# A layer of gated cross-attention and routed experts: the second norm kept as two half-precision parts, an experts' tile's rows transposed by a crossbar DMA

## The reference

```
# x (8, 256, 256), ctx (8, 120, 256), 16 heads of 64; all f32
x = x + tanh(g_xattn) * xattn(layernorm(x), ctx, w_q, w_kv, w_out, b_out)
x = x + tanh(g_ffn)   * ffn(layernorm(x), W1, W2, Wr)

# ffn over T = 2048 rows, E = 8 experts, DFF = 1024, TOPK = 2
probs = softmax(x @ Wr.T);  vals, idx = top_k(probs, 2);  gate = vals / vals.sum
h   = silu(einsum('btd,efd->btef', x, W1))
y   = einsum('btef,edf->bted', h, W2)
out = einsum('bte,bted->btd', gate, y)
```

## Time and profile before

| | us |
|---|---|
| median of 3 runs | 574.97 |
| lowest, highest run | 567.21, 582.94 |
| span of the profiled execution | 560.1 |
| TensorE busy in it | 493.7 |
| VectorE, ScalarE, GpSimd busy | 370.2, 371.3, 363.9 |
| DMA traffic | 93.13 MB, mean 166 GB/s |

### The profile page before, as it was taken

One profiled execution on the slowest core, in us unless ns is written; L12 is line 12 of the kernel. 1 busy time (PEld: TensorE's weight loads), 2 busy tenths in 40 slices (PEclk: granted clock), 3 DMA queues, 4 the chain that ended last, 5 costly groups with the idle time before them and its releaser, 6 DMA issues. The chain is left out here.

```text
span 560.1 us, 17891 instructions
## 1 busy us (share of the span) xinstructions
PE 493.7 (88%) x6630; PEld 438.3 (78%) x6631; DVE 370.2 (66%) x856; ACT 371.3 (66%) x576; POOL 363.9 (65%) x372
## 2 busy tenths in 40 slices
PE   2869799998999999798788997699999999999990
PEld 2757688887888879687567886689898898988980
DVE  5899999898889899699996664343444444343430
ACT  1838999998999899789546674245455464645530
POOL 5466979798989998788978642533544436344531
PEclk9979889999999999999689998799999999999996
DMA  7922506173553625263438598766787877778421
GB/s 286 392 77 84 175 12 219 48 244 59 175 127 119 178 97 168 33 212 73 130 148 201 153 287 145 208 185 186 214 259 201 259 207 232 229 224 244 112 30 17
DMA packets 34846, 93.13 MB, mean 166 GB/s; under 512 B 4967, under 2 KB 24565, under 8 KB 27490
## 3 DMA queue, kind: packets, MB, share of 16 engines
q1 hardware_dynamic: 25634, 81.86, 46.7%
q0 software_dynamic: 8576, 10.30, 9.5%
q10 hardware_dynamic: 576, 0.14, 0.1%
HBM read 74.17 MB, written 18.12 MB: 165 GB/s over the span
## 5 line engine op out<-in xcount | busy, mean ns | idle before, releaser
L689 POOL DMA_INDIRECT out<-yt,row_of x39 | 65.0, 1667 | 115.3 <-DMA out<-yt,row_of 96.5
L1642 PE MATMUL st_bank<-xsT,w_tile 128*128 128x128 f16 x1872 | 114.4, 221 | 4.3 <-issue 3.3
L1480 DVE SCALAR_TENSOR_TENSOR hT<-hf,h_scale,hT 128x512 f16<-128x512 f32 x78 | 58.6, 754 | 88.1 <-ACT hT L974 88.1
L1642 PEld LDWEIGHTS st_bank<-xsT,w_tile 128*128 128x128 f16 x1872 | 109.2, 99 | 7.0 <-issue 5.4
L1642 PE MATMUL o_bank<-w2s,hT 128*128 x936 | 109.9, 274 | 1.2 <-DVE yt L1489 1.1
L1642 PEld LDWEIGHTS o_bank<-w2s,hT 128*128 128x128 f16 x936 | 90.4, 99 | 12.4 <-issue 1.6
L968 ACT ACTIVATE hf<-st_bank,z_scale 128x512 f32<-128x512 f32 x78 | 52.9, 679 | 47.9 <-PE st_bank L1642 40.4
L592 POOL TENSOR_TENSOR pT<-pT 120x512 f16<-120x512 f32 x64 | 77.3, 1221 | 8.0 <-ACT pT L842 7.7
L974 ACT ACTIVATE hT<-hf,h_scale 128x512 f16<-128x512 f32 x78 | 56.3, 722 | 13.1 <-ACT hf L968 4.5
L637 POOL TENSOR_SCALAR stage<-stage,upw 128x512 f32<-128x512 f32 x32 | 55.9, 1748 | 10.5 <-ACT w_hi L941 10.4
L841 ACT ACTIVATE pT<-st_bank,exp_bias,logit_scale 120x512 f32<-120x512 f32 x64 | 50.0, 781 | 12.1 <-PE st_bank L1858 11.6
(11 more groups left out here) (217 smaller groups left out, 966.5 us busy)
## 6 DMA issues: line engine op xcount, KB each, us to landing
w_tile<-w_split SPq DMA_DIRECT2D x39, 1024.0 KB, 5.2
stage<-in_w SPq DMA_DIRECT2D x16, 1024.0 KB, 5.1
w_split<-w_hi SPq DMA_DIRECT2D x8, 512.0 KB, 2.8
w_split<-stage SPq DMA_DIRECT2D x8, 512.0 KB, 3.9
out<-x SPq DMA_DIRECT2D x17, 128.0 KB, 5.4
xin<-in_x SPq DMA_DIRECT2D x8, 256.0 KB, 4.7
w2s<-in_wkv SPq DMA_DIRECT2D x2, 1024.0 KB, 12.2
xres<-in_x SPq DMA_DIRECT2D x16, 128.0 KB
```

The source lines that it names most:

```text
L689: pool.indirect_dma_start(out=out[0:rows], out_offset=bass.IndirectOffsetOnAxis(row_of[:, t:t + 1], 0), in_=yt[t % XG][:], in_offset=None, ...
L1480: nc.vector.scalar_tensor_tensor(out=hT[par][:, 1, 4 * a:4 * a + 4, :], in0=hf[par][:, 512 * a:512 * a + 512].rearrange("p (c n) -> p c n" ...
L1642: ins = pe.matmul(out, lhs[i](a), rhs[i](c), start=(i == 0 and a + c == 0), stop=(i == n - 1 and a == 1))
```

## The change

The rows of the second norm are made in two f16 parts where they are computed. `norm2_factors` scales by `UP_X`, `norm2` (ACT) writes, besides the f32 rows, their high parts to a new tile `xn2p`, and a new step `norm2_low` (POOL) subtracts these from the f32 rows to get the low parts. `store_norm` stores both parts, 1024 bytes a row as before. The gather fetches such rows, and a new step `turn_rows` on SP transposes the gathered 128 x 512 halves with one crossbar DMA, SBUF to SBUF, into `xsT`, which now has four buffers that lie in the dead staging tile `stage[0]`. `up_half` waits for that DMA. The transposes on PE and the two copies on ACT and DVE are gone. A gather now waits for the crossbar DMA of tile t-4 in place of PE's transposes. `norm2_rows` takes the scale back out. The SBUF kept for descriptors of GpSimd's DMAs is halved, to 8192 bytes a partition.

```
+        xn2p = [sb(f"xn2p_{i}", [P, 2, D], F16, att) for i in range(NT)]
-        xsT = [sb(f"xsT{i}", [P, 2, KC, P], F16) for i in range(2)]
-        xg = [sb(f"xg{i}", [P, D], F32) for i in range(XG)]
+        xg = [sb(f"xg{i}", [P, 2 * D], F16) for i in range(XG)]
+        xsT = [stage[0][:, D * i:D * i + D].bitcast(F16).rearrange("p (s k n) -> p s k n", s=2, k=KC) for i in range(XG)]
...
+            def turn_rows(b, t):
+
+                if b != B - 1:
+                    return
+                if t >= XG:
+                    sp.wait_ge(z_full, 2 * (t - XG + 1))
+                sp.wait_ge(xg_in[t % XG], 16 * (t // XG + 1))
+                sp.dma_start_transpose(out=xsT[t % XG].rearrange("p s k n -> p (s k) n"), in_=xg[t % XG][:]).then_inc(xs_in[t % XG], 16)
...
-                sp.wait_ge(xn2_done, 2 * b + t + 1)
-                sp.dma_start(xn2_t[2 * b + t], xn2[t][:]).then_inc(xn2_out[t], 16)
+                sp.wait_ge(xn2_low, 2 * b + t + 1)
+                sp.dma_start(xn2_t[2 * b + t], xn2p[t][:].rearrange("p s d -> p (s d)")).then_inc(xn2_out[t], 16)
...
             for t in range(LISTED, TILES):
                 load_tile(B - 1, t)
+                if t == EARLY + 2:
+                    turn_rows(B - 1, EARLY)
+                    turn_rows(B - 1, EARLY + 1)
+                if t not in (EARLY, EARLY + 1):
+                    turn_rows(B - 1, t)
...
-                chain.link(pool.tensor_scalar(a, a, -0.5, 1.5, ALU.mult, ALU.add))
+                chain.link(pool.tensor_scalar(a, a, -0.5 * UP_X, 1.5 * UP_X, ALU.mult, ALU.add))
...
+            def norm2_low(b, t):
+                if not 0 <= b < B:
+                    return
+                pool.wait_ge(xn2_done, 2 * b + t + 1)
+                pool.wait_ge(xn2_high, 2 * b + t + 1)
+                pool.tensor_tensor(xn2p[t][:, 1, :], xn2[t][:], xn2p[t][:, 0, :], ALU.subtract).then_inc(xn2_low, 1)
...
-                    pool.wait_ge(xs_full, t - XG + 1)
+                    pool.wait_ge(xs_in[t % XG], 16 * (t // XG))
...
+                for t in range(NT):
+                    nc.scalar.activation(xn2p[t][:, 0, :], x2[t][:], ACT.Identity, scale=ln_b[:, 1, t:t + 1],
+                                         bias=ln_b[:, 3, t:t + 1]).then_inc(xn2_high, 1)
...
-            def xs_part(t, par):
-                nc.scalar.activation(xsT[par][:, 0].rearrange("p k n -> p (k n)"), s_bank[par][:, 0:D],
-                                     ACT.Copy, scale=UP_X).then_inc(xs_high, 1)
...
-                nc.vector.tensor_copy(xn2T[:].rearrange("p t k n -> p (t k n)"), src[:]).then_inc(job_free, 1)
+                nc.vector.tensor_scalar(xn2T[:].rearrange("p t k n -> p (t k n)"), src[:], 1.0 / UP_X, None, ALU.mult).then_inc(job_free, 1)
...
-                for kc in range(KC):
-                    ins = pe.transpose(s_bank[par][:, kc * P:(kc + 1) * P], xg[buf][:, kc * P:(kc + 1) * P], ident[:])
...
-                    pe.wait_ge(xs_low, t + 1)
+                    pe.wait_ge(xs_in[buf], before * 16 + 16)
...
-    nc = bacc.Bacc("TRN2", target_bir_lowering=False, num_devices=1)
+    nc = bacc.Bacc("TRN2", target_bir_lowering=False, num_devices=1, dynamic_dma_scratch_size=8192)
```

101 lines of the change are left out of this document (24 added, 77 removed).

## The result

| | before | after |
|---|---|---|
| median of 4 runs each, us | 575.74 | 592.55 |
| lowest, highest | 567.21, 582.94 | 588.29, 593.57 |
| ratio, 95% interval | | 1.043 (1.038 to 1.049) |
| span of the profiled execution | 560.1 | 591.5 |
| the same pair later, on another chip, medians | 566.60 | 581.24 |

The kernel is slower by 3 to 4%. The ratios are of fast executions alone, and leave slow ones out; the medians by themselves give 1.029 and 1.026. The first pair has only four runs of the kernel before, which lie 16 us apart. The page of the kernel after, in parts: busy time and its share, DMA packets, the queues' share of 16 engines' time, and two of the costliest groups (busy, mean ns of one | idle before, releaser).

What follows compares the result with a forecast made beforehand. Back-to-back accumulating scatters, each waiting for the previous landing, were taken to bound the tail. 560 + 2 (attention) + 6 (turn) + 13 (landings) = 581 us; with the 15 us from profile to median, 596 us, range 572 to 630.

Steps and rivals of the forecast that it cites:

- What ends the tail: Tail: scatters run back to back, 5.59 us a tile; taking TensorE's two transposes away is worth 0, only shorter landings help.
- The transfer's own time: Crossbar transpose of 128 KB a tile: takes 1.0 us of the DMA engines, bounds 0.4 and 3.4.
- What it does to the steps: Tail: transpose traffic lengthens each scatter's landing by 0.4 us, times 33, +13 us; bounds 0 and +61.
- The load behind the wait: SP's queue in the tail: load t+1 leaves 6 us later, behind gather t's landing, just ahead of a scatter; priced at nothing.
- The rows' own path: Last tile, gather to products: 6.8 us left for issue and transpose, a transfer takes 3 to 5; fits by 2 us.
- The turn: Attention to experts: SP's wait for gather 2 delays batch 6's stores and the last residual sum; +6 us, bounds 0 and 12.
- The attention stage: Each batch adds 1.45 us to GpSimd and 1.1 to ScalarE, partly covered by spare time; +2 us, bounds 0 and 12.
- The end: Halved memory for GpSimd's DMA descriptors: no row for it, priced at 0.
- From the profile to the median: Whole kernel: profiled execution is 15 us under the runs' median, so the sum of 581 us becomes 596 us.
- The signs: Tail: median landing 5.0 to 5.4 us, steps 6.0, TensorE 0.88, DMA 0.83; SP waits for first gathers; landings of 4.8 or less wrong.

Runs made afterwards that it cites:

- the later order: Changed kernel with every crossbar transpose later in SP's queue, in the tail that of tile t-2 behind the load of tile t: 573.37 us, ratio 1.017.
- e8: Kernel before without TensorE's two f32 transposes of a tile's gathered rows and the copies behind them, nothing in their place: 558.35 us, ratio 0.989.
- e17: Kernel before with one more wait: in the tail SP issues tile t's w_tile load only when the scatter of tile t-6 has landed: 592.29 us, ratio 1.050.
- e1: Kernel before with only the second norm's halves computed, used by nothing, and the smaller descriptor memory: 571.89 us against 565.64.
- e2: Changed kernel with GpSimd's two low-part subtractions moved behind the splitting of w2: 579.38 us, ratio 1.030.
- e15: Changed kernel with both the transposes later in SP's queue and the low-part subtractions later in GpSimd's list: 574.83 us, ratio 1.017.

## Why the prediction was right, and where its steps were not

I said 596 us and slower; it is 592.55. The sum held better than its terms did. Its own difference was +21 us; the two profiles of after have +31.4 and +14.4.

- **What ends the tail.** Right that scatters run one behind another and that their landing sets the step. Wrong in "taking time from TensorE alone cannot end the kernel sooner": without the transposes the step fell by 0.21 us. I had treated the landing as given. It hangs on the load's place, and a load leaves when TensorE has done with a buffer, so TensorE's pace comes back through the landings. The gain is shown, and the loads' places and the landings moved as this way of it wants (0.90 to 1.36 us ahead, 4.82 to 4.61 us); no run holds the one fixed and moves the other. The term was -7 us (33 x 0.21), not 0.
- **The transfer's own time.** I took 1.0 us of the DMA engines between bounds of 0.4 and 3.4; the packets show 0.8 to 1.15. Right. The section "X-Bar Transpose (TRN2)" of the Trainium skill's "Advanced Engine Details and Errata" has it as fast as a regular transfer, which by my estimate from its figure was 0.35 us. The ordinary copy of the same bytes took 0.38 here, the transpose 0.8 to 1.15; the measurement decides. The four 1309 ns of the Trainium skill's "VectorE: DVE Perf Modes", "The three transpose paths", would be 5.2 us one after another, an estimate; the transpose of 484.64 us landed in 3.60 us in full traffic, so they do not add up so here.
- **What it does to the steps.** +0.4 us a landing, 13 us. The mean landing rose by 0.47 us in the first profile and 0.16 in the second, and in the later order the first transpose cost 11 us with its issue and SP's waits: right in size. The mechanism, traffic spread over all landings, is not shown: landings with a transpose and no load beside them stayed at 3.9 to 4.4 us, the median fell, and the long ones were met by loads. (The upper bound should read 1.81 x 33 = 60 us.)
- **The load behind the wait.** "I price this at nothing, having no row for it": this step failed. The rows were there, in the chain of waits that I cite as the earlier trace rows and SP's own timeline side by side: landings of 4.2 to 6.3 us in order of the load's lead. In the change's place, the wait alone costs no less than the whole change, and in the kernel before the load's place alone costs 5%. In the full change the transposes, with 1.2 us of issue each, seem to break that lock up, since scatters of 4.9 us stand beside ones of 7.9; and the wait's share is then smaller than in the kernel with the wait alone. The reordering, which lessens the wait, gains 1 to 2.6%; the whole of it is open.
- **The rows' own path.** "It fits, by 2 us." It does not always: TensorE waited 12 times, 17.1 us in all, for a transpose. I had put the gather at 3.3 us and the transpose at 3 to 5; the gather behind a slow scatter took 5.79. From its issue to the products 9.6 us went by, of the 10.2 that the kernel before had. But these waits are not where the time went: every scatter of the tail left 3.2 us or more after its result.
- **The turn.** +6 us forecast; from the seventh to the eighth batch's norm it is 18.6 us before and 24.7 after. But the two kernels that leave this stretch as before (e8 and e17) have 24.1 and 22.5 there. The first profile's 18.6 was a lucky one, and the agreement is chance. The path that I gave is half there: behind `turn_rows(2)` the stores of batch 6 left 8.7 us after the seventh batch's norm in place of 4.2 ahead of it, and the last residual sum came 16.2 us after that norm in place of 12.95, the 3 us that I said. But in e8 and e17, whose stores leave 6 us ahead, it comes 17.5 and 16.9 us after. The whole turn is 98.6 to 104.0 us in kernels without the halves and 102.7 to 109.9 with them: some 6 us between the means.
- **The attention stage.** +2 us forecast, with 12 as the bound. Kernels without the halves need 157.1 to 158.3 us, those with them 162.6 to 170.7, most of them 165.5 to 165.8: +7.5. It comes with the halves alone (e1), though the smaller memory is in all of these kernels too; their place on GpSimd does not decide it (e2, e15). Which wait carries it is open. My term took the work to be nearly covered by idle time; 2.6 us a batch on two engines that are busy 91 to 93% was covered by less than half: 7.5 us over five batches is 1.5 a batch, about what GpSimd's two subtractions take.
- **The end.** Priced at 0 for want of a row; 6.2 us shorter.
- **From the profile to the median.** I added 15 us, since the profiled execution of before was that much under the median. The profile of after lay 1 us under its own. The sum of 581 was 10 us short of the profiled 591.5, and the 15 us covered that. They belong to that chip and hour: on three later chips the kernel before has medians of 565.16 to 566.60, and the one after 581.24 on one of them. So the nearness of 596 owes much to luck; the ratio that it stands for, 1.037, lies between the two measured.
- **The signs.** Right: the steps (6.11 us for 6.0), TensorE's share of the tail (0.89 for 0.88), the DMA share (0.84 for 0.83), SP's wait for the first gathers. The median landing, 4.45 us, is not the 5.0 to 5.4 that I said, and stands on the side that I called wrong; the mean, 5.29, would fit.

The forecast's mechanism, traffic that slows landings, and the one that it priced at nothing, loads that meet them, come with the same two lines of code, and the runs do not part their shares; TensorE's gain and the shorter end paid for part of both.

## What to carry to other kernels

Where a chain of small transfers ends last, list each one's landing beside the issue time of the nearest large transfer, on whichever queue: if they sort, then anything that shifts the large one (a wait put ahead of it in an in-order queue, a faster engine that frees its buffer) has a price or a gain, before any byte is added. Put a wait for something late behind the loads that need not wait for it. An experiment that takes out half of a change can be slower than the whole, when what is left falls into step with the bound; read its steps before calling its loss a share of the whole. Where a chain of waits names an engine, check that what it names belongs to the same tile. And measure the changed kernel itself again beside the experiments: without that, moving two subtractions would have passed for a gain of 1.3%.

## What the runs showed of the hardware that I had not expected

- A scatter of 128 KB that accumulates lands in 3.8 to 4.2 us with no 1 MB load near, 4.2 with one issued 1.5 us ahead of it, 5.0 at 0.7, and 5.4 to 6.4 with one issued at the same time (before and e17).
- A copy of 128 KB within SBUF in place of a crossbar transpose of the same bytes made the kernel slower (610.94 us against 581 to 593), though SP issues it in 0.47 us and the transpose in 1.22, and its packets take 0.38 us of the 16 engines and the transpose's 0.8 to 1.15.
- In two profiles with transposes the packets of gathers and scatters took 1.6 to 1.7 times as long as without (q0 at 36.4% against 22.8% for nearly the same bytes); in the kernel after, 1.2 times in one profile and 1.7 in the other.
- From the last landing to the end of the span 8.2 us went by in kernels with the full memory for GpSimd's descriptors and some 2 us in those with half of it, with nothing running in either.
